# A gated cross-attention and mixture-of-experts layer: silu on ScalarE from unit 8 on, a shorter route chain, and another order where the small tiles begin

## The reference

```python
scores = softmax(xf @ gate_w.T); topk_w, topk_idx = top_k(scores, 2)   # 4 experts, 2 for each row
g = silu(einsum('nh,eih->eni', xf, eg)); u = einsum('nh,eih->eni', xf, eu)
y = einsum('enh,ne->nh', einsum('eni,ehi->enh', g * u, ed), comb)      # comb: the two shares of each row
y = y + silu(xf @ sg.T) * (xf @ su.T) @ sd.T                           # the shared expert
x = x + tanh(g_ffn) * y
```

## Time and profile before

| | |
|---|---|
| median of three runs | 890.29 us (890.25 to 891.5) |
| the profiled execution | 891.95 us, its span 890.2 us |
| TensorE (PE) busy | 851.2 us, 96% |
| VectorE (DVE) busy | 599.7 us, 67% |
| ScalarE (ACT) busy | 521.2 us, 59% |
| GpSimd (POOL) busy | 459.9 us, 52% |
| mean granted TensorE clock | 0.986 |

### The profile page before, as it was taken

One profiled execution on the slowest core, in us unless ns is written; L12 is line 12 of the kernel. 1 busy time (PEld: TensorE's weight loads), 2 busy tenths in 40 slices (PEclk: granted clock), 3 DMA queues, 4 the chain that ended last, 5 costly groups with the idle time before them and its releaser, 6 DMA issues.

```text
span 890.2 us, 19216 instructions
## 1 busy us (share of the span) xinstructions
PE 851.2 (96%) x6271; PEld 745.9 (84%) x6272; DVE 599.7 (67%) x1259; ACT 521.2 (59%) x1846; POOL 459.9 (52%) x551
## 2 busy tenths in 40 slices
PE   8888999999999898999999999999999999989995
PEld 6566788878888798999988888888888888889994
DVE  6899899999998578878775555555555555434442
ACT  4989999999999343656464544444444544222221
POOL 5686767667665442676431454444444443444442
PEclk9799999999999999999999999999999999999998
DMA  7125223222312222423240333222222222232221
GB/s 217 41 79 175 68 89 93 89 66 91 101 62 85 71 73 68 135 84 119 82 142 24 49 48 48 46 39 41 38 42 42 43 46 36 31 45 45 35 37 22
DMA packets 56889, 62.06 MB, mean 70 GB/s; under 512 B 15643, under 2 KB 45184, under 8 KB 56800
## 3 DMA queue, kind: packets, MB, share of 16 engines
q1 hardware_dynamic: 42871, 43.15, 15.5%
q0 software_dynamic: 12864, 17.57, 12.5%
q10 hardware_dynamic: 1064, 0.21, 0.1%
HBM read 34.78 MB, written 25.82 MB: 68 GB/s over the span
## 4 chain that ended last, share of the span: by engine, by line
PE 82%; DVE 7%; ACT 4%; issue 3%; DMA 2%; POOL 1%; SPq 0%; DVEq 0%; POOLq 0%; ACTq 0%
PE p_s L619 22%; PE p_f L636 12%; PE p_f L2755 8%; PE p_s L339 6%; PE p_f L2800 4%; PE p_s L2755 4%; PE p_t L2686 3%; ACT prob L1478 3%; PE p_s L2672 3%; PE p_t L350 3%; PE p_m L2713 3%; PE p_m L2701 2%; PE p_m L2653 2%; PE p_s L2800 1%; PE p_s L2858 1%
## 5 line engine op out<-in xcount | busy, mean ns | idle before, releaser
L505 POOL DMA_INDIRECT out_rows<-big_yout,slot_id x52 | 86.5, 1664 | 156.4 <-DVE big_yout L582 144.6
L1478 ACT ACTIVATE prob<-p_s,negmax 128x77 f32<-128x77 f32 x512 | 161.2, 372 | 8.2 <-DVE negmax L2023 8.0
L533 ACT ACTIVATE big_sil<-p_s 128x512 f32<-128x512 f32 (+1 forms) x78 | 46.6, 597 | 143.3 <-PE p_s L619 143.3
L1478 ACT ACTIVATION_READ_ACCUMULATOR prob<-p_s,negmax 128x1 f32 x512 | 129.1, 255 | 0.0
L565 DVE TENSOR_TENSOR big_hid<-p_s,big_sil 128x512 f32<-128x512 f32 (+1 forms) x78 | 54.0, 692 | 99.5 <-ACT big_sil L533 99.5
L619 PE MATMUL p_s<-big_fxT_hi,big_w_hi 128*128 128x512 f32 (+1 forms) x286 | 113.9, 398 | 0.2 <-DVE big_w_lo L558 0.2
L619 PE MATMUL p_s<-big_fxT_lo,big_w_hi 128*128 128x512 f32 (+1 forms) x286 | 112.8, 394 | 0.0
L619 PE MATMUL p_s<-big_fxT_hi,big_w_lo 128*128 128x512 f32 (+1 forms) x286 | 112.2, 392 | 0.0
L1104 POOL TENSOR_TENSOR prob<-prob,rinv 128x616 f32<-128x616 f32 x64 | 78.5, 1236 | 62.3 <-DVE rinv L2030 62.3
L1123 POOL TENSOR_TENSOR shT_lo<-shid,shT_hi 128x256 fp32r<-128x256 f32 x80 | 63.2, 801 | 49.3 <-ACT shT_hi L1517 49.0
L636 PE MATMUL p_f<-wd_hi,big_hT_hi 128*128 (+1 forms) x312 | 85.6, 280 | 0.1
(11 more groups left out here) (336 smaller groups left out, 2561.3 us busy)
## 6 DMA issues: line engine op xcount, KB each, us to landing
xr<-in_x SPq DMA_DIRECT2D x16, 256.0 KB, 2.9
x_scratch<-xr SPq DMA_DIRECT2D x16, 256.0 KB, 2.5
xn_scratch<-xn SPq DMA_DIRECT2D x16, 256.0 KB, 2.1
xt_scratch<-xnT SPq DMA_DIRECT2D x16, 256.0 KB, 2.6
xin<-xt_scratch SPq DMA_DIRECT2D x16, 256.0 KB, 3.6
x1in<-x_scratch SPq DMA_DIRECT2D x16, 256.0 KB, 3.3
out_rows<-syout SPq DMA_DIRECT2D x16, 256.0 KB, 2.4
raw<-in_L_ffn_ed SPq DMA_DIRECT2D x4, 688.0 KB, 4.4
```

The costliest lines, as they stand in the source:

```text
L505: pool.indirect_dma_start(out, bass.IndirectOffsetOnAxis(slot_id[:, column(j, t)], 0), yout[:, t, :], None, compute_op=ALU.add).then_inc(s ...
L533: act.activation(sil[n % 2][0:r, :], p_gu[c % 2][0][0:r, :], ACT.Silu).then_inc(s_sil, 1)
L1478: last = act.activation(prob[n % 2][t][:, m * PW + h * SK:m * PW + (h + 1) * SK], p_s[:, 2 * t + h // 4, col:col + SK], ACT.Exp, bias=negm ...
```

## The change

From unit 8 on (`SILU`) ScalarE applies silu itself to the gate, VectorE only multiplies by up, and `result` takes the whole `tgf`. The route chain is cut: running sums are scans of one instruction, two additions are folded into others, and the copy of `base` comes later. Its order changes: `weights` and `counts` go into unit 8 (and `bases` on TensorE before `gate_up(8, 4)`), `starts` before `inner(9, 0)`, `position` and `tiles_and_rows` between the `inner`s of unit 9 behind `result(8)`, and `experts_of_tiles` from unit 14 to unit 11. Where the small tiles begin, TensorE does only half of `big_down(12, 4)` before `gate_up(0)` of the small tiles and the rest behind it; the last `big_result`s come behind `hid(0)` on VectorE; the hidden tile's first four chunks go to the fourth bank of `p_s` and its last two to `p_f[0]`, so that `hidden_T(0)` waits for the first two results only, and that ahead of chunk 4; `gather(2, 0)` goes ahead of the last block's adds.

```diff
@@ small tiles: on_gpsimd, on_vector, hidden_T, run
-        gather(2, 0)
         for j in range(2):
             gather(j + 3, 1 - j)
             add(j, j)
...
-    def on_vector(dve):
+    def on_vector(dve, last_results):
...
                                     sil[:, CUT:FF].unsqueeze(1).broadcast_to(twice), ALU.mult).then_inc(s_dup, 1)
+            if isinstance(j, int) and j == 0:
+                last_results()
             if not last:
                 x_lo(j + 1)
...
-        def hidden_T(j):
+        def hidden_T(j, second_bank=None):
             pe.wait_ge(s_hid, j + 1)
             wait(pe, s_hlo, j)
             for c in range(FC):
+                if c == 4 and second_bank:
+                    second_bank()
...
-        def run(gate_banks, hidden_banks):
-            gate_banks()
+        def run(banks_of_gate, last_of_blocks, bank_of_hidden):
+            banks_of_gate()
 
             def step(j, k):
                 fixed = isinstance(j, int)
                 gate_up(j, expert(k))
+                if fixed and j == 0:
+                    last_of_blocks()
...
-                    if fixed and j == 0:
-                        hidden_banks()
-                    hidden_T(j)
+                    hidden_T(j, bank_of_hidden if fixed and j == 0 else None)
@@ wide blocks: down takes t0, t1
-            for t in range(BT):
+            for t in range(t0, t1):
@@ banks handed to small_tiles
-                           (p_s[:, 0:GUB, :].rearrange("p b n -> p (b n)"), p_m, p_f, p_t), s_add)
+                           (p_s[:, 0:GUB, :].rearrange("p b n -> p (b n)"), p_m, (p_s[:, 3, :], p_f[0]), p_t), s_add)
@@ GpSimd, wide blocks
                     small_gather(0, 0)
                     small_gather(1, 1)
+                if j == NB - 1:
+                    small_gather(2, 0)
                 big_adds(j)
@@ ScalarE gate, VectorE inner and result (SILU = LATE + 1)
-                act.activation(th[0:r, (FC * n + c) % 4, :], f_bank(n, c)[0:r, 0:UT * P], ACT.Tanh,
-                               scale=0.5).then_inc(s_th, 1)
+                share, bank = th[0:r, (FC * n + c) % 4, :], f_bank(n, c)[0:r, 0:UT * P]
+                if n < SILU:
+                    act.activation(share, bank, ACT.Tanh, scale=0.5).then_inc(s_th, 1)
+                else:
+                    act.activation(share, bank, ACT.Silu).then_inc(s_th, 1)
...
-                nc.vector.scalar_tensor_tensor(out=half_gate, in0=half_gate, scalar=1.0, in1=bank[0:r, 0:UT * P],
-                                               op0=ALU.add, op1=ALU.mult).then_inc(s_ah, 1)
-                dve.wait_ge(s_ah, FC * n + c + 1)
+                if n < SILU:
+                    nc.vector.scalar_tensor_tensor(out=half_gate, in0=half_gate, scalar=1.0, in1=bank[0:r, 0:UT * P],
+                                                   op0=ALU.add, op1=ALU.mult).then_inc(s_ah, 1)
+                    dve.wait_ge(s_ah, FC * n + c + 1)
...
-                                               scalar=tgfh[:, :], in1=x1in[:, n % 2, :, :], op0=ALU.mult,
+                                               scalar=(tgfh if n < SILU else tgf)[:, :], in1=x1in[:, n % 2, :, :], op0=ALU.mult,
@@ VectorE route chain: starts, numbered, experts_of_tiles
-                for e in range(1, E):
-                    link(tt(blocks[:, e:e + 1], blocks[:, e - 1:e], blocks[:, e:e + 1], ALU.add))
-                link(ts(big_end[:, :], blocks[:, :], float(NB), float(WIDE), ALU.min, ALU.mult))
-                link(tt(rest_n[:, :], count[:, :], big_end[:, :], ALU.subtract))
+                link(nc.vector.tensor_tensor_scan(big_end[:, :], fresh[0][:, 0:E], blocks[:, :], 0.0, ALU.mult, ALU.add))
+                link(ts(big_end[:, :], big_end[:, :], float(NB), float(WIDE), ALU.min, ALU.mult))
+                link(nc.vector.scalar_tensor_tensor(out=rest_n[:, :], in0=count[:, :], scalar=float(P - 1),
+                                                    in1=big_end[:, :], op0=ALU.add, op1=ALU.subtract))
                 link(tt(rest_n[:, 1:E], rest_n[:, 1:E], big_end[:, 0:E - 1], ALU.add))
-                link(ts(rest_n[:, :], rest_n[:, :], float(P - 1), None, ALU.add))
...
-                for e in range(1, E):
-                    link(tt(small_at[:, e:e + 1], small_at[:, e - 1:e], rest_n[:, e - 1:e], ALU.add))
+                link(nc.vector.tensor_tensor_scan(small_at[:, 1:E], fresh[0][:, 0:E - 1], rest_n[:, 0:E - 1], 0.0,
+                                                  ALU.mult, ALU.add))
...
-                link(ts(base[:, :], base[:, :], -1.0, None, ALU.add))
+                link(nc.vector.tensor_copy(base[:, :], p_t[:, 0:E]))
...
-                link(tt(cum[:, :, :], cum[:, :, :], base[:, :].unsqueeze(2).broadcast_to(wide_e), ALU.add))
+                link(nc.vector.scalar_tensor_tensor(out=cum[:, :, :], in0=cum[:, :, :], scalar=-1.0,
+                                                    in1=base[:, :].unsqueeze(2).broadcast_to(wide_e),
+                                                    op0=ALU.add, op1=ALU.add))
...
+                for a, b, ends in ((0, NB, big_end[0:1, 0:E - 1]), (NB, NX, small_at[0:1, 1:E])):
+                    link(ts(te[:, a:b], tile_at[:, a:b], ends[:, 0:1], None, ALU.is_ge))
+                    for e in range(1, E - 1):
+                        link(nc.vector.scalar_tensor_tensor(out=te[:, a:b], in0=tile_at[:, a:b], scalar=ends[:, e:e + 1],
+                                                            in1=te[:, a:b], op0=ALU.is_ge, op1=ALU.add))
@@ VectorE order in units 8, 9, 11 and 14
                 inner(8, 3)
+                weights()
                 inner(8, 4)
                 e_lo(3)
+                counts()
                 inner(8, 5)
                 e_lo(4)
 
                 last_lo(8)
-                weights()
+                starts()
                 inner(9, 0)
-                counts()
-                starts()
                 inner(9, 1)
                 numbered()
-                position(0)
-                position(1)
-                tiles_and_rows()
                 result(8)
                 inner(9, 2)
+                position(0)
                 inner(9, 3)
+                position(1)
                 e_lo(5)
                 inner(9, 4)
+                tiles_and_rows()
                 inner(9, 5)
                 e_lo(6)
...
                 rows_at(2)
+                experts_of_tiles()
                 inner(11, 0)
...
                 e_lo(21)
-                experts_of_tiles()
                 places(7)
@@ VectorE and TensorE at the end of the wide blocks
-            for t in range(BT):
-                big_result(NB - 1, t)
-            late["vector"](dve)
+
+            def last_results():
+                for t in range(BT):
+                    big_result(NB - 1, t)
+
+            late["vector"](dve, last_results)
...
                 gate_up(8, 3)
+                bases()
                 gate_up(8, 4)
                 e_T(3)
                 gate_up(8, 5)
-                bases()
...
-            big_down(NB - 1, FC - 2)
-            big_down(NB - 1, FC - 1)
-            late["tensor"](pe)(lambda: pe.wait_ge(s_hid, FC * (NU + NB)), lambda: pe.wait_ge(s_y, NU + 2 * NB))
+
+            def banks_of_gate():
+                pe.wait_ge(s_hid, FC * (NU + NB))
+
+            def last_of_blocks():
+                big_down(NB - 1, FC - 2, BT // 2, BT)
+                big_down(NB - 1, FC - 1)
+
+            def bank_of_hidden():
+                pe.wait_ge(s_y, NU + 2 * NB - 1)
+
+            big_down(NB - 1, FC - 2, 0, BT // 2)
+            late["tensor"](pe)(banks_of_gate, last_of_blocks, bank_of_hidden)
```

More of the change, by code:

```diff
@@ L68 @@
 LATE = (NU + 2 - FIRST) // 2
+SILU = LATE + 1
 SB0 = 16512
@@ L621, in gate_up, with down @@
             last.then_inc(s_gu, 1)
-        def down(j, c):
+        def down(j, c, t0=0, t1=BT):
             n = FC * j + c
@@ L778, in attend_share_route @@
         w_parts = [sb(f"w_{s}", [P, NE], f32r) for s in ("hi", "lo")]
-        tile_at, te, hit = (sb(n, [1, NX]) for n in ("tile_at", "te", "hit"))
+        tile_at, te = (sb(n, [1, NX]) for n in ("tile_at", "te"))
         spare = sb("spare", [P, NS])
@@ L2355, in counts @@
                 dve.wait_ge(s_base, 1)
-                link(nc.vector.tensor_copy(base[:, :], p_t[:, 0:E]))
                 link(nc.vector.tensor_copy(count[:, :], p_t[:, E:2 * E]))
@@ L2404, in experts_of_tiles @@
                 link(nc.vector.tensor_copy(tile_at[:, :], tile_at_i[:, :]))
-                for e in range(1, E):
-                    into = te if e == 1 else hit
-                    link(ts(into[:, 0:NB], tile_at[:, 0:NB], big_end[0:1, e - 1:e], None, ALU.is_ge))
-                    link(ts(into[:, NB:NX], tile_at[:, NB:NX], small_at[0:1, e:e + 1], None, ALU.is_ge))
-                    if e > 1:
-                        link(tt(te[:, :], te[:, :], hit[:, :], ALU.add))
+                for a, b, ends in ((0, NB, big_end[0:1, 0:E - 1]), (NB, NX, small_at[0:1, 1:E])):
```

(1 more changed line is left out.)

## The result

| | before | after |
|---|---|---|
| median of four runs | 890.38 us (890.25 to 891.5) | 881.86 us (881.17 to 883.88) |
| the profiled execution | 891.95 us | 881.68 us |
| its span | 890.2 us | 879.9 us |
| mean granted TensorE clock | 0.986 | 0.992 |

A forecast was written before the change was run, and what follows sets the result against it. TensorE, busy 96% of the span, was taken as the bound, so only its waits counted: 5.2 + 1.1 + 4.3 = 10.6 us off 891.95 gives 881.35, carried to the median as 879.7 us; range 878.0 to 883.2.

The forecast's parts named there:

- The likeliest case: The forecast itself, all gains as counted: 878.3 to 881.0 us, chance 0.62.
- A: Unit 9's route chain: TensorE's waits for shid and syout and the lower clock go, worth 5.2 us.
- B: Unit 14's wait for at_row behind the expert table: moving the table to unit 11 gives 1.1 us, between 0 and 1.15.
- the slack: Unit 9: result(8) starts near 349.0 us, TensorE wants it at 352.7, so the wait has 3.7 us to spare.
- rival 1: Unit 9: VectorE still late, its links held while GpSimd works, up to 2.8 us lost, 882.5 us; chance 0.13.
- The silu: Units 8 to 15: saves VectorE 21.6 us, ScalarE's cost unchanged, moved table load free; only makes cover elsewhere.
- Rival 4: Units 8 to 15: silu alternating with copies brings repeated table loads, slower, 956 us with twelve a unit; chance 0.02.
- C: Handover from the last wide block to the first small tiles: earlier gather and new order give 4.3 us.
- Rival 2: Handover: the clock still falls after new waits summing to 1.7 us, costing 1.7 us, 881.4 us; chance 0.14.
- Rivals 3 and 5: Only the handover pays, 886.0 us, chance 0.05; silu slower from PSUM or partial gains, under 1.8 us, chance 0.02.
- The clock: Granted clock no longer falling: 1.7 us counted in unit 9 and 1.8 us in the handover.
- From the profile to the median: The profiled execution before stood 1.66 us above the median; carried over, 881.35 us became 879.7 us.

The follow-up runs named there:

- e9: The changed kernel with tiles_and_rows behind last_lo(9) on VectorE and low_shares(7) ahead of h_lo(14, 0) on GpSimd: 881.57 us, ratio 0.9899 to before.
- e8: The changed kernel with experts_of_tiles back in unit 14: 881.99 us, ratio 0.9900 to before.
- e1: The kernel before with ScalarE's silu alone in units 8 to 15: 889.04 us, ratio 0.9983 to before.
- e2: The kernel before with the shorter, reordered route chain and experts_of_tiles in unit 11, still tanh: 888.98 us, ratio 0.9985 to before.
- e6: The kernel before with unread transposes, 16 ahead of gate_up(9, 5) and 14 ahead of the small tiles' x_T(2): 888.06 us, ratio 0.9965 to before.
- e7: The changed kernel with gather(2, 0) back behind the last block's adds: 890.87 us, ratio 1.0002 to before.
- e11: The changed kernel with two late-unit steps moved, last results split around x_lo(1), and gather(3, 1) ahead of the adds: 881.16 us, ratio 0.9889 to before.

## Why the prediction was right, and where it was not

The forecast was 879.7 us, the range 878.0 to 883.2; measured were 881.86. The likeliest case came about in the main: no wait for `shid` or `syout`, none for the rows of `gather(2, 0)`, no fall of the clock in the two places. Two of its signs did not: unit 9 has a wait above 0.5 us, for `e_lo(6)`, and where `at_row` was waited for, `at_val` is. The sum was made against the profiled execution, 891.95 - 10.6 = 881.35, and the profiled execution of after took 881.68. That it is so close is partly luck: 1.0 us of the difference lies in attention, for which the forecast had nothing. In the stages that the change touches 9.3 us were gained of 10.6, and 3.1 of the 9.3 are there only because the profiled execution of before had both falls.

**A and B: 6.3 us forecast, 5.25 measured.** `result(8)` was put near 349.0 us, and it starts at 349.00, which is luck: attention ended 1.0 us sooner in this execution, so against the first landmark it moved up by 5.7 us (from 44.58 to 38.90 behind it) and not by 6.7. These rows show its end, and links that took longer than I had counted:

```profile
345.83 0.42 DVE L2055 TENSOR_TENSOR shid<-p_f,th 128x256 f32<-128x256 f32 x1 [1.31 <-ACT th L1518]
346.17 0.87 DVE L2393 SCALAR_TENSOR_TENSOR cum<-cum,base 128x128 f32<-128x128 f32 x1
347.07 0.81 DVE L2397 TENSOR_TENSOR ttmp<-cum,big_end 128x128 f32<-128x128 f32 x1
347.92 0.72 DVE L2398 TENSOR_TENSOR ttmp<-ttmp,jump 128x128 f32<-128x128 f32 x1
348.67 0.29 DVE L2399 TENSOR_TENSOR cum<-cum,ttmp 128x128 f32<-128x128 f32 x1
349.00 0.75 DVE L2068 SCALAR_TENSOR_TENSOR syout<-p_s,tgf,x1in 128x512 f32<-128x512 f32 x1
...
353.36 0.69 DVE L2406 CAST pos_i<-posf 128x64 int32<-128x64 f32 x1
354.09 0.67 DVE L2407 TENSOR_SCALAR til_i<-pos_i 128x64 int32<-128x64 int32 x1
354.79 0.20 DVE L2408 TENSOR_SCALAR row_i<-pos_i 128x64 int32<-128x64 int32 x1
```

GpSimd at the same time:

```profile
345.61 1.29 POOL L1121 TENSOR_TENSOR xnT_lo<-xin,xnT_hi 128x512 fp32r<-128x512 f32 x1 [4.30 <-ACT xnT_hi L1508]
347.00 1.49 POOL L1127 TENSOR_TENSOR shT_lo<-shid,shT_hi 128x256 fp32r<-128x256 f32 x2
352.57 2.13 POOL L1127 TENSOR_TENSOR shT_lo<-shid,shT_hi 128x256 fp32r<-128x256 f32 x3 [4.08 <-ACT shT_hi L1526]
```

The links of `numbered` beside GpSimd took 0.7 to 0.9 us, the one behind it 0.29. Links of 64 columns in `tiles_and_rows` took 0.69 and 0.67 us beside GpSimd, and 0.20 right behind. In `numbered` the slack took it in, as the forecast said, but it was less than the 3.7 us. That figure set the start of `result(8)` against the moment at which TensorE wants its end, and so left out the 0.75 us that it runs. In after `result(8)` ends at 349.75 us and `gate_up(9, 5)` starts at 351.31: 1.6 us to spare.

In `tiles_and_rows` there was no slack. The failed step is "following the two engines' orders by hand I get about 0.3 us of wait": it was 1.09 us, for `e_lo(6)`. The two held links are some 1.0 us too long (0.69 + 0.67 - 2 x 0.20), as much as the wait, so here rival 1 came true at a little over a third of its price. e9 shows that it was `tiles_and_rows` in that place, and its rows say that GpSimd held it: the same `pos_i` and `til_i` take 0.20 us each there, begun while GpSimd is idle, and `row_i`, 0.20 us in after, takes 1.26 us beside GpSimd's 1.29. No run takes GpSimd's instruction away to show it outright. The Trainium skill ("SBUF — State Buffer", Who interferes with whom) has the loser of such a contention blocked for the whole of the other's instruction. The prediction had named the links with two SBUF inputs; those of `numbered` were held, but so were `pos_i`, `til_i` and `big_end`, which have one. The rows agree that VectorE is held, `big_end` of the earlier trace rows for as long as GpSimd's own 1.29 us; the links here were held for 0.5 us each beside GpSimd instructions of some 0.7 us, so what it cost was the part that was left of them.

The bound of B was right and the choice in it was not. I took 1.1 of 0 to 1.15 us. But `spread(7)` needs `low_shares(7)` too, which stands behind `h_lo(14, 0)` in GpSimd's queue and ended 0.72 us after TensorE wanted it: the gain in B is 0.4 us. Nor did it need the move of the table (e8): silu alone brings `at_row` early enough (e1), and the route chain's part, with the move in it, does so too (e2).

**The silu** took 0.38 us for 256 columns, no more than tanh; one table load shows, of 1.28 us, at 327.53 us between the last step of unit 7 and the first silu, and TensorE has no wait from 320 to 340 us, so it cost nothing. Rival 4 had asked for a load at each turn; there is none behind that one. (Its sum was loose: six loads a unit would already have lost (6 x 1.28 - 5.8) x 8 = 15 us, more than the 10.6, and not only seven.)

**C: 4.3 us forecast, 4.0 measured.** `gate_up(1)` was to start 3.23 us after `hid(0)`: it starts 773.14 - 770.06 = 3.08 us after it. The three new waits of about 0.2, 0.5 and 1.0 us are two, of 0.33 and 0.78; `x_T(2)` doesn't wait, and `x_T(3)` hardly does, as `gather(3, 1)` began at 780.89, 2.91 us ahead of it. Rival 2 did not come about in any of the nine profiled executions with the new handover and `gather(2, 0)` in front. Rivals 3 and 5 fell with the stage table: the late units gave more than the handover.

**The clock** was about right in size (1.5 us in unit 9 instead of 1.7; in C 1.6 us, where the 1.8 us had been the whole of the lost pace) and wrong in kind: I counted it as a property of the waits, and the same waits have it in one execution and not in another.

**From the profile to the median** is the step that missed most. The profiled execution of before stood 1.66 us above its median and I carried that over; after's stood 0.18 us below its own, and that makes 1.84 of the 2.2 us by which the forecast was too low. A single execution's distance from the median doesn't belong to the kernel: the untouched attention stage alone varies by 3.5 us.

## What to carry to other kernels

Follow every queue that a releaser stands in, not only the one that is late now: of the two waits that were left in after, both were a step of another engine in a slightly wrong place, and moving two lines took them away. Instructions saved on an engine that is not the bottleneck are worth little by themselves and more together with an order that uses them (1.7 and 2.8 us here, for 48 multiply-adds); measure the parts on the others' background too. Where a change of a few us is to be judged, compare stages between landmarks of the bound engine: a stage that is not disturbed repeats to 0.1 us, the whole only to 2 or 3. Look at the granted clock of each stage before taking its difference for the edit's: a fall in one of the two executions is 1.5 us of it, and a fall in the baseline is no gain to count on.

## What the runs showed of the hardware

- A VectorE instruction of 64 to 128 columns took 0.67 to 0.87 us beside GpSimd's arithmetic, and 0.20 to 0.29 us behind it; in e9 one of 64 columns took 1.26 us beside a GpSimd instruction of 1.29.
- The same pair of waits of TensorE (1.20 and 2.58 us) was followed by a granted clock of 0.57 in one execution and of 1.00 in another; with some 1.9 us of useless transposes within the longer wait it was 1.00 in the one trace taken.
- Attention, with the same instructions, took 310.1 to 313.6 us. Part of it is the clock: from 40 to 50 us it was granted at 0.83 in before and 1.00 in after. These are the rows of before and after:

```profile
40.00:50.00 10.00, 9.29 (x76) 6.14 (x76) 8.63 (x17) 8.99 (x55) 6.78 (x6) 0.83 0.38 114
```

```profile
40.00:50.00 10.00, 8.42 (x81) 5.91 (x80) 9.33 (x19) 10.00 (x60) 6.78 (x6) 1.00 0.39 127
```

- The rows of a gather that TensorE waited for landed 2.8 to 2.9 us after it began (before, e1, e2, e6, e7), and once 3.50 us (e11).
